# Turning operands by SP's transposing loads instead of TensorE, and the experts' products in two PSUM banks

## What is computed

```python
scores = x @ w + b;  x = x[top 88 of 125 per sequence]         # token selection
h = layernorm(x)
qkv = fq_act(h @ fq_weight(w_qkv).T + b_qkv)                   # 12 heads of 16
attn = fq_act(q @ k.T * Dh ** -0.5)
p = log_int_softmax(attn)                                      # powers of two, 4 bits
o = fq_act(p @ v);  x = x + fq_act(o @ fq_weight(w_proj).T + b_proj)
t = rmsnorm(layernorm(x)) * scale;  g = t @ gate_w.T + gate_b  # 16 experts, best 4 of each token
y = swiglu(t @ w1[e] + b1[e]) @ w2[e] + b2[e]
out = x + sum over the chosen e of softmax(g)[e] * y[e]
```

## Time and profile before

| | us |
|---|---|
| median of 3 runs (lowest, highest) | 760.58 (757.69, 761.43) |
| profiled execution, its own time | 765.98 |
| its span in the trace | 764.2 |

### The profile page before, as it was taken

One profiled execution on the slowest core, in us unless ns is written; L12 is line 12 of the kernel. 1 busy time (PEld: TensorE's weight loads), 2 busy tenths in 40 slices (PEclk: granted clock), 3 DMA queues, 4 the chain that ended last, 5 costly groups with the idle time before them and its releaser, 6 DMA issues.

```text
span 764.2 us, 14352 instructions
## 1 busy us (share of the span) xinstructions
PE 441.1 (58%) x3943; PEld 294.3 (39%) x3943; DVE 560.7 (73%) x1426; ACT 490.9 (64%) x874; POOL 447.3 (59%) x554
## 2 busy tenths in 40 slices
PE   0695353746456463745633335567687787788454
PEld 0242132333334242433422224345465565466343
DVE  3686897899999999898998645545676665666746
ACT  0055876798897969788774535255666655666664
POOL 9781725247587987979777653555455444445500
PEclk9997555555555555555555567679999988979669
DMA  9469999999011030210101164425444344431078
GB/s 186 55 145 293 318 318 294 321 293 285 13 55 53 22 93 30 79 40 6 51 11 40 52 102 86 101 72 126 97 92 93 83 95 86 91 81 34 1 291 317
DMA packets 149613, 93.65 MB, mean 123 GB/s; under 512 B 77122, under 2 KB 143643, under 8 KB 149538
## 3 DMA queue, kind: packets, MB, share of 16 engines
q1 hardware_dynamic: 139266, 75.04, 38.7%
q0 software_dynamic: 10272, 17.70, 7.3%
HBM read 23.61 MB, written 61.24 MB: 111 GB/s over the span
## 4 chain that ended last, share of the span: by engine, by line
PE 22%; ACT 18%; SPq 17%; DVE 17%; issue 12%; another core or an unknown queue 6%; POOL 4%; DMA 2%; DVEq 0%; ACTq 0%; POOLq 0%
SPq L483 7%; PE pX L1920 6%; PE pS L1904 6%; PE pP L1904 4%; SPq L475 3%; POOL w1s L597 2%; DVE S_e L1462 2%; ACT stage L1059 2%; DVE negmx L1381 2%; SPq L537 2%; DMA w2s<-expert_rows 2%; SPq L432 2%; PE pP L1796 1%; ACT stage L1044 1%
## 5 line engine op out<-in xcount | busy, mean ns | idle before, releaser
L782 POOL DMA_INDIRECT expert_rows<-stage,dest x118 | 118.6, 1005 | 130.3 <-ACT stage L1044 74.4
L1593 DVE TENSOR_SCALAR arena<-pS 128x512 f32<-128x512 f32 x59 | 40.6, 689 | 80.7 <-remote 59.9
L1920 PE MATMUL pX<-w2s,stage 128*128 x472 | 65.1, 270 | 39.8 <-ACT stage L1044 32.1
L706 POOL DMA_INDIRECT region<-rows,slots x60 | 68.0, 1134 | 16.5 <-issue 15.9
L597 POOL TENSOR_TENSOR w1s<-stage,w1s 128x384 f16<-128x384 f32 (+8 forms) x72 | 67.3, 935 | 11.4 <-ACT w1s L866 6.4
L1920 PEld LDWEIGHTS pX<-w2s,stage 128*128 128x128 f16 x472 | 43.6, 106 | 57.3 <-issue 53.6
L1052 ACT ACTIVATE arena<-pS 64x256 f32<-64x256 f32 x59 | 22.1, 375 | 59.5 <-PE pP L1904 30.1
L1796 PE MATMUL pP<-idb,S_p 128*88 128x128 bf16 x192 | 25.8, 316 | 46.3 <-DVE S_p L1414 46.3
L1674 PE MATMUL pX<-arena,WA 128*128 128x384 f16 x86 | 34.4, 501 | 30.5 <-ACT arena L878 21.2
L1823 PE MATMUL pP<-WpT,oq 128*128 128x192 bf16 x72 | 15.4, 349 | 60.7 <-ACT pTs L996 57.7
L706 POOL DMA_INDIRECT region<-arena,slots x36 | 41.0, 1138 | 15.6 <-issue 8.5
(11 more groups left out here) (442 smaller groups left out, 1620.7 us busy)
## 6 DMA issues: line engine op xcount, KB each, us to landing
region<-zrow SPq DMA_DIRECT2D x45, 800.0 KB
w1s<-expert_rows SPq DMA_DIRECT2D x16, 384.0 KB, 7.7
stage<-in_L_ffn_w_dram SPq DMA_DIRECT2D x24, 192.0 KB
stage<-in_L_ffn_w_dram SPq DMA_DIRECT2D x8, 384.0 KB
w2s<-expert_rows SPq DMA_DIRECT2D x8, 384.0 KB, 11.8
arena<-in_x_dram SPq DMA_DIRECT2D x4, 672.0 KB
expert_rows<-stage,dest POOLq DMA_INDIRECT x118
out_dram<-xsel SPq DMA_DIRECT2D x8, 198.0 KB
```

Of the source, the lines that this page charges most:

```text
L706: pool.indirect_dma_start(region_rows, bass.IndirectOffsetOnAxis(ap=slots[q % 3][:, i, m:m + 1], axis=0), rows[q % 3][:, i, :].bitcast(I16 ...
L782: pool.indirect_dma_start(y_dram, bass.IndirectOffsetOnAxis(ap=dest[(st - 7) % 8][:, j:j + 1], axis=0), ysb[b][:, j, :], None, bounds_chec ...
L1593: dve.tensor_scalar(lin[r], hidLC[r], -6.0 * XS * WS, 8.0 * XS * WS, ALU.max, ALU.min).then_inc(s["l_done"], 1)
L1920: ins = pe.matmul(y_ps[:, j, :], lhs, w2s[:, kind, bass.ds(k_, 1), :].rearrange("p o f -> p (o f)"), start=n == 0, stop=n == 4)
```

## The change

- `turn_x_by_load`: for quads 3 to 7 (`XQ = 3`) SP turns x by six transposing loads from SBUF to SBUF, in its slot 6, 9, 12, 15 or 18, in place of nine PE transposes and six DVE copies. `project_qk` waits for `x_turned`.
- `turn_by_load`: for quads 0 to 6 SP turns the router's rows by three transposing loads, in place of nine PE transposes and two DVE copies. ACT's `last_rows` and PE's `gate_rows` wait for `turned`.
- `turn_p`: from slot 7 on (`PT_AT = 7`; 18 slots) SP turns `S_p` by one transposing load into `pTs`, in place of twelve PE transposes and two ACT copies. `S_p` becomes 128 wide per head for it. PE's product with v waits for `p_turned`.
- SP's loop runs over slots and issues these loads between the loads of the weights; the kinds of halves in `xT` and `xTr` stand in another order.
- `y_ps` alternates between banks pX and pO from step 7 on (`Y_APART`), so PE waits for the copy of the step before last.
- Small tables (`own`, `packf` and others) lie in `S_u`, to make room.

```diff
-        y_ps = pX[:, 0:2 * C].rearrange("p (j c) -> p j c", j=2)
+        y_banks = [bank[:, 0:2 * C].rearrange("p (j c) -> p j c", j=2) for bank in (pX, pO)]
+        def y_ps(n):
+            return y_banks[n % 2 if n >= Y_APART else 0]
...
-            for m in range(2, E // 2 + 1):
-                for f in range(*((0, 24) if m == 2 else (24, 34) if m == 3 else (34, NFILL) if m == 4 else (0, 0))):
-                    fill_rows(f)
-                if m < E // 2:
+            def turn_x_by_load(q):
+                sp.wait_ge(s["low1"], 2 * q + 2)
+                sp.wait_ge(s["xr_filled"], fill(3 * q - 4, "v", 1) + 1)
+                for i in range(3):
+                    for rows_, at, m in ((slice(0, MAIN), MAIN * i, MAIN), (slice(MAIN, 128), 3 * MAIN + TAIL * i, TAIL)):
+                        sp.dma_start(xT[:, :, at:at + m], xw[rows_, i, :], transpose=True).then_inc(s["x_turned"], 16)
+            def turn_by_load(q):
+                sp.wait_ge(s["low2"], 2 * q + 2)
+                if q >= 1:
+                    sp.wait_ge(s["xr_filled"], fill("gate", q - 1) + 1)
+                    sp.wait_ge(s["ter_copied"], q)
+                for i in range(3):
+                    sp.dma_start(xTr[:, :, 128 * i:128 * i + 128], rows[q % 3][:, i, 0:2 * C],
+                                 transpose=True).then_inc(s["turned"], 16)
+            def turn_p(st):
+                if st == PT_AT:
+                    sp.wait_ge(s["pads_zeroed"], 3)
+                sp.wait_ge(s["p_ready"], st)
+                sp.wait_ge(s["o_ready"], st - 1)
+                sp.dma_start(pTs[:, :, :], S_p[:, :, :].rearrange("p h n -> p (h n)").bitcast(BF16),
+                             transpose=True).then_inc(s["p_turned"], 16)
+            for st in range(NT + 1):
+                m = st // 3 + 2
+                if st % 3 == 0 and XQ <= m - 1 < NQ:
+                    turn_x_by_load(m - 1)
+                if st % 3 == 1 and m >= 4:
+                    turn_by_load(m - 4)
+                if st >= PT_AT:
+                    turn_p(st)
+                if st % 3 == 1 and m < E // 2:
+                    if m < 4:
+                        for f in range(*((0, 24), (24, 34))[m - 2]):
+                            fill_rows(f)
                     sp.wait_ge(s["stage_low"], 12 * (m - 1))
                     load_pair(m % 2, 2 * m)
+                    if m == 3:
+                        for f in range(34, NFILL):
+                            fill_rows(f)
+            turn_by_load(LASTQ - 1)
...
                     if st >= 6:
-                        pe.wait_ge(s["y_out"], p - 5)
+                        pe.wait_ge(s["y_out"], p - 5 if st - 5 <= Y_APART else p - 6)
```

More of the change, by code:

```diff
@@ L729, in _ @@
             pool.wait_ge(s["extra_low"], 3)
+            pool.wait_ge(s["gathered"], NQ)
+            pool.memset(S_p[:, :, KEEP:128], 0.0).then_inc(s["pads_zeroed"], 1)
             def slot(st, n, q):
@@ L1043, in gate_values @@
                         act.wait_ge(y_sent[b], it * 64 + 32 * ((u - 6) // 4))
-                    act.activation(ysb[b], y_ps, ACT.Copy, scale=1.0 / (XS * WS * WS)).then_inc(s["y_out"], 1)
+                    act.activation(ysb[b], y_ps(st - 6), ACT.Copy, scale=1.0 / (XS * WS * WS)).then_inc(s["y_out"], 1)
                 if active(st, 2):
@@ L1411, in slot @@
                     dve.wait_ge(s["rb_ready"], n)
-                    if st >= 2:
+                    if st > PT_AT:
+                        dve.wait_ge(s["p_turned"], 16 * (n - PT_AT))
+                    elif st >= 2:
                         dve.wait_ge(s["pT_ready"], 2 * n - 2)
-                    dve.tensor_scalar(S_p[:, :, :], S_rb[:, :, :].bitcast(I16), -1, 0x7F80, ALU.bitwise_xor,
+                    dve.tensor_scalar(S_p[:, :, 0:KEEP], S_rb[:, :, :].bitcast(I16), -1, 0x7F80, ALU.bitwise_xor,
                                       ALU.bitwise_and).then_inc(s["p_ready"], 1)
-                if nxt and i == 0:
+                if nxt and i == 0 and q + 1 < XQ:
                     evac_xT(1, fill(st, "x", 1))
@@ L1681, in project_v @@
                     i = 2 * h + b
-                    for kind, W in enumerate((WA, WA, WD)):
-                        pe.matmul(bank[:, b, :], xT[:, kind, MAIN * i:MAIN * i + MAIN], W[:, 768:768 + C], start=kind == 0, stop=False)
+                    for n, (kind, W) in enumerate(((0, WA), (2, WA), (1, WD))):
+                        pe.matmul(bank[:, b, :], xT[:, kind, MAIN * i:MAIN * i + MAIN], W[:, 768:768 + C], start=n == 0, stop=False)
                     ins = pe.matmul(bank[:, b, :], one_of[:, :].broadcast_to([128, MAIN]), v_rows, start=False, stop=True)
@@ L1720, in turn_rows @@
                     src, cols = rows[q % 3][:, i, :], slice(128 * (i % 2), 128 * (i % 2) + 128)
-                    for kind, lo in enumerate((0, 2 * CA, CA)):
-                        ins = pe.transpose(turned(q)[m][:, kind, cols], src[:, lo:lo + 128], idh[:, :])
+                    for kind, lo in enumerate((0, CA, 2 * CA)):
+                        ins = pe.transpose(rT_last[m][:, kind, cols], src[:, lo:lo + 128], idh[:, :])
                 ins.then_inc(s["xr_filled"], 1)
@@ L1727, in gate_rows @@
                 pe.wait_ge(s["ter_copied"], q + 1)
[L1728 removed]
+                if q < LASTQ:
+                    pe.wait_ge(s["turned"], 48 * q + 48)
+                else:
+                    pe.wait_ge(s["tT_drained"], 2)
                 pe.wait_ge(s["xr_drained"], fill("gate", q))
@@ L1795, in slot @@
                     for h in range(8):
-                        ins = pe.transpose(pP[0:KEEP, 0, 128 * h:128 * h + 128], S_p[:, h, :].bitcast(BF16), idb[:, :])
+                        ins = pe.transpose(pP[0:KEEP, 0, 128 * h:128 * h + 128], S_p[:, h, 0:KEEP].bitcast(BF16), idb[:, :])
                     ins.then_inc(s["pT_ready"], 1)
@@ L1800, in slot @@
                     for h in range(8, 12):
-                        ins = pe.transpose(pP[0:KEEP, 1, 128 * (h - 8):128 * (h - 8) + 128], S_p[:, h, :].bitcast(BF16),
+                        ins = pe.transpose(pP[0:KEEP, 1, 128 * (h - 8):128 * (h - 8) + 128], S_p[:, h, 0:KEEP].bitcast(BF16),
                                            idb[:, :])
                     ins.then_inc(s["pT_ready"], 1)
-                if nxt and i == 0:
+                if nxt and i == 0 and q + 1 < XQ:
                     transpose_x(2, fill(st, "x", 2))
@@ L1809, in slot @@
                     rank_rows(quad_at(st, RANK))
-                if quad_at(st, TURN) is not None:
-                    for m in range(2):
-                        turn_rows(quad_at(st, TURN), m)
                 if nxt and i == 1:
```

86 lines of the change are left out of this document (48 added, 38 removed).

## The result

| | us | ratio to before |
|---|---|---|
| before, median of 4 runs | 761.0 (757.69 to 763.13) | |
| changed, median of 4 runs | 780.67 (777.08 to 782.65) | 1.0257 (95%: 1.0203 to 1.0311) |
| changed, profiled execution | 782.65, span 780.9 | |

What follows compares the result with a forecast made beforehand. Attention was taken as bound by a three-engine loop of 44.3 us a quad, the experts by PE's gaps. From 766.0, +11.6 + 6 - 23 gave 760.6; less 5.4 for the profiled execution's excess, 755.2 us, range 740 to 774.

Steps and rivals of the forecast that it cites:

- Term 1: Quad 3's first projection: x turned by SP comes late behind the stores of zeros, +11.6 us.
- Term 2: Router's slots: SP's turns of rows and `S_p` delay the experts' choice, 1.2 us a quad for five quads, +6 us.
- I scale the issue by size and keep the 2.3: SP's turns in router slots: issue 0.62 us per small turn, 2.46 for `S_p`, landing 2.3 us after issue.
- -1.4 on the other side: Router's slots, per quad: DVE's 1.00 us wait at L1241 and about 0.4 of copies go.
- DVE's remaining waits have one place: the first instruction of `top_experts`: Attention, kernel before: DVE's remaining waits stand only at the choice of experts, which recurs every 44.3 us.
- Followed back, its time is set by a loop over three engines: Attention: the choice's period is set by a loop through softmax, low halves and turned rows, 17.5 + 21.3 + 5.5 = 44.3 us.
- What the removed work is worth: Attention: the copies and transposes taken from DVE, ACT and PE gain only what the router's term already has.
- term of 0 for `S_p` in the other slots: Slots without router turns: `S_p`'s turn lands at 259.2, hidden by 1.6 us before the product at 260.79, so no cost.
- Term 3: Experts' loop: two banks remove PE's 18 waits for ACT's copy, -23 us (-8 to -30).
- dear loads: Rival, chance 0.14: issue from SBUF costs twice, 1.23 us a small turn and 4.9 for `S_p`; 776 to 786 us.
- The experts' wait only changes its name: Rival, chance 0.22: PE waits for ACT's gate function or clamps instead, the banks give 8.5 us; 769.7 us.
- serial blocks: Rival, chance 0.02: each 128 x 128 block costs 1.23 us, so SP's queue bounds attention; about 875 us.

Runs made afterwards that it cites:

- experiment 3: Changed kernel with SP's turn of quad 3's x moved into the zeros' stores: 699.05 us in S; with all three groups of turns out of the stores' way: 693.16.
- experiment 6: POOL makes the rows' low halves after 8 of 12 weight pieces, in L: kernel before with two banks 750.78 us (0.988); changed kernel 766.51 (1.006 of before).
- experiment 7: Changed kernel with spread zeros and early low halves, in S: 667.93 and 667.51 us (0.988); PE's turns instead, 671.39; only `S_p` left to PE and ACT, 668.29.
- S: Group of runs, on four chips, in which the kernel before takes 676 us; the changed kernel takes 703.28 us there, ratio 1.043.
- L: Group of runs, all of one chip apart from the first measurement, in which the kernel before takes 761 us; the changed kernel rerun there takes 777.73, ratio 1.022.

## Why the prediction was wrong

It forecast 5.4 us less and the profiled execution takes 16.7 more: 22 us apart.

- **Term 1, the stall (11.6 forecast, 13.5 measured).** The place was right, and so was the queue behind the stores. PE had x of quad 3 at 190.0 instead of 187.5, inside the bounds, but not for the reason given. The prediction took the zeros' drain as the end of the wait and six issues of a few times 0.3 us as hidden in it. The stores were down by 185, and the six issues took 9.79 us, until 188.7. Not seen was that the rows' and `S_p`'s turns were stalled too: it cost nothing here, yet it hides most of what mending x alone would give (experiment 3).
- **Term 2, the router (+6 forecast, +14.8 measured over slots 8 to 23).** The step that failed is "I scale the issue by size and keep the 2.3". A small turn costs 1.26 us and not 0.62, `S_p` 1.46 and not 2.46, and `S_p` then lands in 2.7. From the low halves to the choice the sum was 8.1, the trace has 9.1. The -1.4 on the other side was overrated too: of 3.6 us the period kept 2.7. I named the product with v and the gates' product as queued behind SP's turns and left out ACT, which stands at L957 for 5.2 us with a quantization and the softmax's root behind it.
- **"DVE's remaining waits have one place: the first instruction of `top_experts`".** This reading was wrong. The earlier trace rows show no wait there. DVE's waits over slots 8 to 23 of the kernel before (191.5 to 411.9 us; total, times, longest) stand at the copies of turned rows and at L1241, 14.2 us with three smaller ones, and none at L1309:

```profile
DVE early L1300 <- PE pX L1722: 6.5, 10, 1.7
DVE arena L1241 <- PE pX L1684: 5.0, 5, 1.0
```

  In the changed kernel the choice does wait, in each of the five quads (205 to 440 us):

```profile
DVE arena L1360 <- PE pX L1792: 31.6, 5, 8.2
DVE S_e L1511 <- ACT S_sq L1039: 2.8, 4, 1.2
```

  34.4 us of waits instead of 14.2 is 20.2 more, and the stretch is 14.8 longer: DVE lost some 5.4 us of other time and more than lost it again at the choice.
- **"Followed back, its time is set by a loop over three engines".** This was not shown by the sum 17.5 + 21.3 + 5.5 = 44.3: any path from one choice to the next adds up to the period. With the low halves 5.8 us earlier, the old kernel's choice came 1.0 us earlier in that quad (experiment 6). In the changed kernel the loop does bind, since SP's turn hangs on the low halves and PE's work in front of it is gone; there the same edit makes slot 23 start 14.4 us earlier.
- **"What the removed work is worth": nothing beyond term 2.** Right for the changed kernel as it stands. DVE waits 5.68 us at the choice. Once neither stall nor low halves are in the way, SP's turns are worth 3.9 us against PE's (experiment 7). The term of 0 for `S_p` in the other slots holds in that nothing else was late: PE waits 2.95 us for it at 275.6, and in that quad DVE waits only at the choice and 0.5 us at `S_e`.
- **Term 3, the banks (-23 forecast, -12.1 between the two traces, -9.3 with the end).** The step that failed is the choice of the whole 23.6, the waits taken as time gained, where the low bound was 8. From 537 us on the waits are gone, and the time did not fall by them. The prediction had PE's share of the loop over 82%, and it is (83%); the step from there to 23 us failed. In S the banks give 1.1 to 1.7 us, measured four times, and the traces show why: there POOL has no time left. That the end after the loop grows when POOL's scatters run later was in no term.

Of the rivals, "dear loads" (776 to 786) has the measured 780.67 in its range, and by luck. Its small turn is right (1.23 against 1.26) and its `S_p` is not (4.9 against 1.46), so it had attention's loss at 39 us or more for the measured 28, and it kept the 23 us of term 3: two errors that cancel. "The experts' wait only changes its name" (769.7) had the banks' size, 8.5 against 9.3 net, but not its reason as far as S shows it, where the loop waits for POOL; and it had attention's loss at 17.6.

How much the banks give in L is not settled. Two sums of medians put it at about 7 to 12 us. If the loads cost 28 to 29 us in L as they do in S, where the change with one bank takes 28.4 to 28.8 more, and the whole change costs 17 to 20, the banks give 9 to 12. Banks with early low halves gain 10.3 in L (experiment 6), of which some 3 are attention, which leaves 7. Single traces can't: the loop from the first product to the 58th takes 226.7 to 235.5 us in the five profiled executions with two banks in L, against 247.6 in the one with one bank, so another execution alone moves it by 9. Why the loop is longer in L is open.

The Trainium skill's page "VectorE: DVE Perf Modes", section "The three transpose paths", has 1309 ns for a block of 128 x 128 through the DMA. As a price for each block, which the rival "serial blocks" made of it, the trace disagrees from SBUF too: `S_p`'s 12 blocks land 4.1 us after the issue begins, 0.34 each. No run here times a block alone. The rule in its section "Rules for kernel authors", TensorE where a result in PSUM will do, came out right for the change as it stands, and no longer once SP's queue was put in order and the low halves came early (3.9 us).

## What to carry to other kernels

Before a load is given a job on the critical path, count the loads, not the bytes: here each cost its queue 1.2 to 1.5 us, and whatever stands ahead of it in that queue (here 11 stores that wait for bandwidth) is its delay. When a wait is removed, look for the second chain that ends at the same point: of 13.5 us of stall 4 came back when one of three queued groups was moved and 10 when all were. A wait's total is not what its removal gives: here it gave about half in one pair of traces, and in the other group, where another engine had no idle time, hardly any. And a path that adds up to the period proves nothing: look for the waits of the engine at its end.

## What the runs showed of the hardware

- Transposing loads from SBUF to SBUF issue in 1.26 us (six of 7.6 us, three of 3.8), hardly less for small ones: `S_p` whole 1.46, half 1.29. Behind queued stores the same six took 8.4 to 10.1.
- The same program took 761 us in one group of runs and 676 in the other, with the difference in the experts' stage. With one bank PE was busy for 77% of 120 us of its loop in the one and 93% in the other, and its register instructions at w1's weights took up to 747 ns against 46. A ratio for the change (1.022 to 1.026, and 1.043) holds for its group alone.
- POOL's indirect stores of a step's results follow each other with a gap of about 0.3 us. In the faster group they and POOL's other work filled the loop: 132.2 us busy and 31.3 of such gaps in 171.7.
